# Expert layer of a routed feed-forward block: first product transposed, with its weights streamed per tile as the stationary operand, second matrices resident

## What is computed

```python
k_logits, k_index = jax.lax.top_k(logits, TOPK)
k_prob = jax.nn.softmax(k_logits, axis=-1)
for e in range(E):
    we = jnp.sum(jnp.where(k_index_f == e, k_prob_f, 0.0), axis=-1)
    h = jax.nn.silu(xf @ w1[e] + b1[e]) @ w2[e] + b2[e]
    out = out + we[:, None] * h
x = x + gb * out
```

## Time and profile before

| | us |
|---|---|
| median of 3 runs | 2193.87 |
| lowest and highest of them | 2185.4, 2199.5 |
| span of the profiled execution | 2187.8 |
| experts: from the first DMA issue to the end | 1582.3 to 2187.8 |

### The profile page before, as it was taken

How to read it: one execution, slowest core, us unless ns; L and a number is a source line. 1 busy time by engine, 2 the same in 40 slices (tenths; PEclk the granted TensorE clock), 3 DMA queues, 4 the chain that set the end, 5 groups by cost and what they waited for, 6 DMA issues and landing times. The chain is left out here.

```text
span 2187.8 us, 35435 instructions
## 1 busy us (share of the span) xinstructions
PE 1909.5 (87%) x9314; PEld 1097.2 (50%) x9315; DVE 1300.8 (59%) x2620; ACT 1282.9 (59%) x1387; POOL 357.6 (16%) x383
## 2 busy tenths in 40 slices
PE   2988199898999999989799996699089999999998
PEld 1433044444444444444344445588056667776665
DVE  5543177676877777777577774765234444444443
ACT  4323099898998989989799992244012222222222
POOL 1330200100001000000000003215501111111111
PEclk7988599999999999999899998899589999999999
DMA  3455661506033060521605204622262112222211
GB/s 122 153 171 199 152 152 43 107 10 125 23 71 82 19 130 5 101 52 40 108 5 101 53 6 127 200 116 79 89 190 34 32 31 34 34 34 34 34 31 25
DMA packets 139177, 172.28 MB, mean 79 GB/s; under 512 B 16672, under 2 KB 89248, under 8 KB 138976
## 3 DMA queue, kind: packets, MB, share of 16 engines
q1 hardware_dynamic: 116672, 143.00, 26.6%
q0 software_dynamic: 13824, 19.03, 5.0%
q10 hardware_dynamic: 8608, 9.47, 1.3%
HBM read 106.42 MB, written 65.03 MB: 78 GB/s over the span
## 5 line engine op out<-in xcount | busy, mean ns | idle before, releaser
L771 DVE SCALAR_TENSOR_TENSOR probs<-probs,scal,bil_ps 128x512 f32<-128x512 f32 (+1 forms) x1152 | 773.6, 715 | 278.5 <-ACT probs L734 169.6
L734 ACT ACTIVATE probs<-raw_ps 128x2048 f32<-128x2048 f32 (+1 forms) x288 | 518.7, 1801 | 84.3 <-PE raw_ps L669 84.3
L741 ACT ACTIVATE probs<-probs 128x2048 f32<-128x2048 f32 (+1 forms) x288 | 529.7, 1839 | 34.8 <-DVE probs L771 34.8
L681 PE MATMUL bil_ps<-u_mv,w_st 128*128 128x512 f32 (+3 forms) x1280 | 469.9, 426 | 54.1 <-DVE probs L771 30.8
L1442 ACT ACTIVATE hid_t<-h_tr_ps,b 128x128 f32<-128x128 f32 x576 | 156.3, 383 | 475.7 <-PE h_tr_ps L1406 409.6
L681 PEld LDWEIGHTS bil_ps<-u_mv,w_st 128*128 128x128 f32 x1280 | 217.3, 192 | 410.5 <-DVE probs L771 380.8
L669 PE MATMUL raw_ps<-q_mv,k_st 128*128 128x512 f32 (+3 forms) x1280 | 337.1, 390 | 52.8 <-DMA v_sb<-v_rows 45.1
L696 PE MATMUL o_ps<-probs,v_sb 128*32 128x512 f32 (+3 forms) x2560 | 298.5, 548 | 0.5 <-POOL probs L654 0.5
L669 PEld LDWEIGHTS raw_ps<-q_mv,k_st 128*128 128x128 f32 x1280 | 212.3, 194 | 143.9 <-ACT probs L734 70.1
L1397 PE MATMUL fc_ps<-w,rows_t 128*128 x576 | 262.1, 598 | 1.2 <-issue 0.6
L1417 PE MATMUL fc_ps<-w,hid_t 128*128 x1152 | 260.9, 380 | 1.7 <-DMA b<-in_b 0.9
(11 more groups left out here) (186 smaller groups left out, 1313.7 us busy)
## 6 DMA issues: line engine op xcount, KB each, us to landing
q_mv<-q_split SPq DMA_DIRECT2D x128, 128.0 KB
rows<-x_rows SPq DMA_DIRECT2D x72, 130.0 KB, 2.1
v_rows<-v_st SPq DMA_DIRECT2D x8, 1024.0 KB, 5.2
k_st<-k_split SPq DMA_DIRECT2D x64, 128.0 KB
k_st<-k_split SPq DMA_DIRECT2D x128, 64.0 KB
v_sb<-v_rows SPq DMA_DIRECT2D x32, 256.0 KB
o_t<-o_sb SPq DMA_DIRECT2D x32, 256.0 KB, 2.2
o_t_sb<-o_t SPq DMA_DIRECT2D x32, 256.0 KB, 2.8
```

Of the source, the lines that this page charges most:

```text
L681: mm = pe.matmul(bil_ps[:, hd % 2, column:column + width], w_st[:, kt * P:(kt + 1) * P], u_mv[:, hd, qb * BLK + query:qb * BLK + query + w ...
L734: act.activation(probs[:, s % NBUF, :, first:BLK], raw_ps[:, :, first:BLK], ACT.Tanh).then_inc(tanh_ready, 1)
L741: act.activation(scores, scores, ACT.Exp).then_inc(exp_ready, 1)
L771: dve.scalar_tensor_tensor(scores, scores, scal[:, ALPHA:ALPHA + 1], bil_ps[:, hd % 2, first:BLK], ALU.mult, ALU.add).then_inc(sum_ready, 1)
```

## The change

- **First product.** Eight groups (`hc`) of two matmuls (`k`): the 128x128 piece of `w1` is the stationary operand, the transposed rows (128 columns) are the moving one. The result in `fc1_ps` has the hidden units on partitions, so the eight transposes of `hid`, the copy to `hid` and `h_tr_ps` are gone; SiLU reads `fc1_ps`. The pipeline has three parts instead of four.
- **Weights.** `w2` is loaded whole in the router stage, in the place of `w1`. `w1` is loaded for each tile by SP, 1 MB of the tile's expert, to one of WB = 4 buffers, right behind the tile's rows. SP waits for the first product of tile m-4 besides its waits of before.
- **Buffers.** `fc1_ps` and `fc2_ps` have two buffers each.
- **VectorE's order.** The probabilities of tile m are read right after the copy of `rows_t`, ahead of the sums of tile m-2.
- TensorE's loop holds four steps instead of two.

The diff, cut to its core:

```diff
-            w1v = w1[:, :].rearrange("p (e k n) -> p e k n", e=E, k=KC)
+            w2v = w2[:, :].rearrange("p (e c n) -> p e c n", e=E, c=HID // P)
             for e in range(E):
-                sp.dma_start(w1v[:, e], a["w1"][e].rearrange("(k p) n -> p k n", p=P)).then_inc(w1_in, 16)
+                sp.dma_start(w2v[:, e], a["w2"][e].rearrange("(c p) n -> p c n", p=P)).then_inc(w2_in, 16)
...
+        WB = 4
+        w1 = sb("w1", [P, WB, KC, HID])
-        hid = sb("hid", [P, 2, HID])
-        fc1_ps = ps("fc1_ps", [P, HID])
-        h_tr_ps = ps("h_tr_ps", [P, HID])
-        fc2_ps = ps("fc2_ps", [P, BLK])
+        fc1_ps = ps("fc1_ps", [P, 2, HID])
+        fc2_ps = ps("fc2_ps", [P, 2, BLK])
...
         def _(sp):
                 if active(0):
+                    sp.wait_ge(fc1_mm, m + (FC1_0 - WB + 1))
                     sp.wait_ge(x_tr_mm, m + (XTR_0 - 1))
                     sp.wait_ge(meta_ready, m + (META_0 - 1))
                     row = sp.value_load(tile_row[0:1, ds(m, 1)], min_val=0, max_val=VOID)
                     sp.dma_start(rows[:, u % 2, :], dram["x_rows"][ds(row, P), :]).then_inc(rows_in[u % 2], 16)
+                    e = sp.value_load(tile_expert[0:1, ds(m, 1)], min_val=0, max_val=E - 1)
+                    src = a["w1"].rearrange("e (k p) n -> e p k n", p=P)[ds(e, 1), :, :, :]
+                    sp.dma_start(w1[:, u % WB, :, :], src.rearrange("z p k n -> (z p) k n")
+                                 ).then_inc(w1_in[u % WB], 16)
...
         def _(pe):
                 if active(1):
+                    pe.wait_ge(w1_in[q], (n // WB) * 16 + 16)
                     pe.wait_ge(rows_t_ready, n + (RT_0 + 1))
-                    pe.wait_ge(hid_ready, n + HID_0)
-                    for half in range(HID // BLK):
+                    pe.wait_ge(hid_t_ready, n + (HT_0 - 1))
+                    for hc in range(HC):
                         for k in range(KC):
-                            mm = pe.matmul(fc1_ps[:, half * BLK:(half + 1) * BLK], rows_t[:, p, k * P:(k + 1) * P],
-                                           w1[:, ds(e * (KC * HID) + (k * HID + half * BLK), BLK)],
-                                           start=(k == 0), stop=(k == KC - 1))
+                            mm = pe.matmul(fc1_ps[:, p, hc * P:(hc + 1) * P], w1[:, q, k, hc * P:(hc + 1) * P],
+                                           rows_t[:, p, k * P:(k + 1) * P], start=(k == 0), stop=(k == KC - 1))
...
-                    for hc in range(HC):
-                        tr = pe.transpose(h_tr_ps[:, hc * P:(hc + 1) * P], hid[:, p, hc * P:(hc + 1) * P],
-                                          ident[:, :])
-                    tr.then_inc(h_tr_mm, 1)
-                if active(3):
...
-            skewed(pe, NET, 3, 2, step)
+            skewed(pe, NET, 2, WB, step)
...
         def _(act):
-            for e in range(E):
-                act.dma_start(w2v[:, e], a["w2"][e].rearrange("(c p) n -> p c n", p=P)).then_inc(w2_in, 16)
             act.dma_start(b2[:, :], a["b2"].partition_broadcast(P)).then_inc(w2_in, 16)
...
-                        silu = act.activation(hid_t[:, p, cols], h_tr_ps[:, cols], ACT.Silu,
+                        silu = act.activation(hid_t[:, p, cols], fc1_ps[:, p, cols], ACT.Silu,
...
         def _(dve):
-                    dve.wait_ge(fc1_mm, n + (FC1_0 + 1))
-                    dve.wait_ge(h_tr_mm, n + (HTR_0 - 1))
-                    dve.tensor_copy(hid[:, p, :], fc1_ps[:, :]).then_inc(hid_ready, 1)
```

More of the change, by code:

```diff
@@ L155, in build @@
                          rw1, router_weights, pad_base, tile_first, x_back)
-            stage_router(nc, a, dram, modrow, ident, rows_sb, stats2, rstd2, token_f, blank, w1, w1_in, out,
+            stage_router(nc, a, dram, modrow, ident, rows_sb, stats2, rstd2, token_f, blank, w2, w2_in, out,
                          router_weights, pad_base, tile_first, tile_expert, expert_f, tile_row, pad_row)
-        stage_experts(nc, a, dram, modrow, ident, tile_expert, expert_f, tile_row, w1, w1_in,
+        stage_experts(nc, a, dram, modrow, ident, tile_expert, expert_f, tile_row, w2, w2_in,
                       out)
@@ L984, in _, with stage_router @@
             dve.scalar_tensor_tensor(pairs[:, :, 0], pairs[:, :, 0], -1.0, rstd2[:, :], ALU.mult, ALU.mult)
-def stage_router(nc, a, dram, modrow, ident, rows_sb, stats2, rstd2, token_f, blank, w1, w1_in, out,
+def stage_router(nc, a, dram, modrow, ident, rows_sb, stats2, rstd2, token_f, blank, w2, w2_in, out,
                  router_weights, pad_base, tile_first, tile_expert, expert_f, tile_row, pad_row):
@@ L1328, in stage_experts @@
         x_tr_ps = ps("x_tr_ps", [P, BLK])
-        fc1_ps = ps("fc1_ps", [P, HID])
-        h_tr_ps = ps("h_tr_ps", [P, HID])
-        fc2_ps = ps("fc2_ps", [P, BLK])
+        fc1_ps = ps("fc1_ps", [P, 2, HID])
+        fc2_ps = ps("fc2_ps", [P, 2, BLK])
         rows_in = [sem(f"rows_in{p}") for p in range(2)]
-        b1_in, w2_in = sem("b1_in"), sem("w2_in")
+        w1_in = [sem(f"w1_in{p}") for p in range(WB)]
+        b1_in = sem("b1_in")
         added, y_free = sem("added"), sem("y_free")
@@ L1414, in step @@
                     pe.wait_ge(hid_t_ready, n + (HT_0 + 1))
-                    pe.wait_ge(y_sum_ready, n + YS_0)
+                    pe.wait_ge(y_sum_ready, n + (YS_0 - 1))
                     for hc in range(HC):
-                        mm = pe.matmul(fc2_ps[:, 0:D], hid_t[:, p, hc * P:(hc + 1) * P],
+                        mm = pe.matmul(fc2_ps[:, p, 0:D], hid_t[:, p, hc * P:(hc + 1) * P],
                                        w2[:, ds(e * (HC * D) + hc * D, D)], start=(hc == 0), stop=(hc == HC - 1))
                     mm.then_inc(fc2_mm, 1)
-            skewed(pe, NET, 3, 2, step)
+            skewed(pe, NET, 2, WB, step)
         @block.scalar
@@ L1434, in step @@
             def step(m, u, active):
[L1435 to L1437 removed]
+                if active(1):
+                    n, p = m - 1, (u - 1) % 2
+                    act.wait_ge(fc1_mm, n + (FC1_0 + 1))
                     act.wait_ge(fc2_mm, n + (FC2_0 - 1))
@@ L1441, in step @@
                         cols = slice(hc * P, (hc + 1) * P)
-                        silu = act.activation(hid_t[:, p, cols], h_tr_ps[:, cols], ACT.Silu,
+                        silu = act.activation(hid_t[:, p, cols], fc1_ps[:, p, cols], ACT.Silu,
                                               bias=b1[:, ds(e * HC + hc, 1)])
                     silu.then_inc(hid_t_ready, 1)
-            skewed(act, NET, 2, 2, step)
+            skewed(act, NET, 1, 2, step)
         @block.vector
@@ L1467, in step @@
                     dve.tensor_copy(rows_t[:, u % 2, :], x_tr_ps[:, 0:D]).then_inc(rows_t_ready, 1)
-                if active(1):
-                    n, p = m - 1, (u - 1) % 2
-                    dve.wait_ge(fc1_mm, n + (FC1_0 + 1))
-                    dve.wait_ge(h_tr_mm, n + (HTR_0 - 1))
-                    dve.tensor_copy(hid[:, p, :], fc1_ps[:, :]).then_inc(hid_ready, 1)
[L1473 to L1487, removed]
                     k = u % TR
@@ L1501, in step @@
                                       ).then_inc(meta_ready, 1)
-            skewed(dve, NET, 3, TR, step)
+                if active(2):
+                    n, p, k = m - 2, u % 2, (u - 2) % TR
+                    e = expert_of(n)
+                    dve.wait_ge(meta_ready, n + (META_0 + 1))
+                    dve.wait_ge(y_ready, n + Y_0)
+                    dve.scalar_tensor_tensor(gate[:, :], gates[1], late[:, k:k + 1], gates[0],
+                                             ALU.mult, ALU.add).then_inc(gate_ready, 1)
+                    dve.wait_ge(fc2_mm, n + (FC2_0 + 1))
+                    dve.wait_ge(y_free, n + (FREE_0 - 1))
+                    dve.tensor_tensor(y[:, p, :], fc2_ps[:, p, 0:D], b2[:, ds(e * D, D)], ALU.add
+                                      ).then_inc(y_sum_ready, 1)
+                    dve.wait_ge(gate_ready, n + 1)
+                    dve.wait_ge(y_sum_ready, n + (YS_0 + 1))
+                    dve.scalar_tensor_tensor(y[:, p, :], y[:, p, :], share[:, 1, k:k + 1], gate[:, :],
+                                             ALU.mult, ALU.mult).then_inc(y_ready, 1)
+            skewed(dve, NET, 2, TR, step)
 INPUTS = ["x", "c_t", "wmod", "ident", "scalars", "transforms", "transform_weights", "qkv_wt", "code_wt",
```

30 lines of the change are left out of this document (9 added, 21 removed).

## The result

| | before | after |
|---|---|---|
| median of 4 runs, us | 2190.6 | 2129.05 |
| lowest and highest, us | 2185.4, 2199.5 | 2123.47, 2134.5 |
| span of the profiled execution, us | 2187.8 | 2129.3 |
| experts, from their first DMA issue to the end of the span, us | 605.5 | 544.4 |

The ratio after to before is 0.9725, with an interval of 0.9697 to 0.9754 (the two medians alone give 0.9719, inside it): faster by 2.5 to 3.0%. The forecast was 2130 us.

A forecast was written before the change was run, and what follows sets the result against it. TensorE alone was taken to bound the experts. Start 1591.7, products 504.7, transposes 15.4, clock 1.7 and end 10.9 gave a 2124.4 us span, 63.4 less; off the 2193.9 median, 2130 us (2112 to 2150; 2168 with the accumulation case).

The forecast's parts named there:

- The bound: Experts' steady part: TensorE alone binds, at clock 1.00, with a step of 7.99 us before the change.
- The step: TensorE's step: eight transposes go (-0.87 us), first product takes 3.55 us for 3.44; 7.23 us for 7.99.
- The rivals with a pitch of 0.133 and of 0.19: First product's 32 records: at 0.133 us apart, 2181 us in all (6%); at 0.19, loads unhidden, 2312 us (8%).
- What must stay hidden: Work beside TensorE's step, such as SiLU, y, accumulations, row and weight loads: all stays hidden, cost 0.
- the estimate of 3.3 us a megabyte: Weight stream: 1 MB takes 3.3 us at 316 GB/s; with old traffic 4.9 of 7.23 us, share near 0.68.
- the rival's mechanism: GpSimd's accumulation, delayed some 3.0 us by the weight burst, sets a 7.7 us step: 34 us more, 2164 us; 10%.
- the phase: Within a step: accumulation data move from 3.7 to 6.0 us; weights are issued at 4.6 and move towards their landing.
- The router: Router stage: loading 8 MB of w2 in 1 KB pieces instead of w1 in 4 KB pieces costs 0.
- The start: Start of experts: first product of tile 0 at 1591.7 us (1593.4 before), its second near 1601 instead of 1614.4.
- My 1.7: First product of tile 0: TensorE's lower clock of 1.2 GHz adds 1.7 us over the steady one.
- The end: From the last matmul to the end of the span: 10.9 us, where it was 10.0 before.
- The sum: Whole kernel: 2124.4 us of span, 63.4 less than 2187.8; taken off the median of 2193.9, 2130 us.

The follow-up runs named there:

- 2 MB: Changed kernel with each w1 tile loaded twice, the second time to buffers that TensorE waits for but doesn't use: 2123.7 us, the experts 545.8.
- a full collision: Changed kernel with each w1 tile issued when the y of an earlier tile is ready, so its 1 MB moves during that accumulation: 2120.8 us.
- 2.5 MB: Changed kernel with each tile's weights loaded twice and half of them a third time, to an unread DRAM buffer: 2187.67 us, the experts 580.5.
- The two runs with a better start: Changed kernel with the first four w1 tiles loaded in the router stage: ratio to before 0.9727; the same with b2 moved behind tile 1's transposes: 0.9752.
- the yardstick: The changed kernel again, unaltered, on two occasions: 2139.14 and 2135.96 us, ratios to before 0.9706 and 0.9727.

## Why the prediction was right, point by point

**The bound.** TensorE's step sets the experts, before and after, without a gap and at clock 1.00. Shown by the profile after, and by the run with the old product, whose step is that of before.

**The step.** Forecast 0.22 + 3.55 + 3.46 = 7.23, measured 0.22 + 3.57 + 3.46 = 7.25. The pitch of the 32 records is 0.1116 us where 0.111 was taken. The 64-column run shows that it is the load, and not the streaming (0.107), that sets this pitch, and so that the reading of the earlier trace rows and of the loads in the earlier trace rows (0.110 and 0.113) was sound, while the 0.133 from the matmul row was too high, as suspected. The rivals with a pitch of 0.133 and of 0.19 are excluded: in a run of 32 as in one of 4 the next load begins before the record of the one before it ends, and only 0.004 us of each stand out over the streaming. The 0.76 x 72 = 55 us of the forecast are the 53 to 56 between the old and the new product.

**What must stay hidden.** Costed at nothing, and the run without the stream confirms it to about 1 us. The margin was mis-sized on both sides: the estimate of 3.3 us a megabyte made 2 MB impossible, and they fit. But the rival's mechanism is real. It is the accumulation's landing, one at a time on GpSimd, that ends the room: 4.0 us with the stream as placed, 6.0 under a full collision, 5.7 with 2 MB, 6.7 with 2.5 MB. The reason given against it, the phase (issues 2.2 us apart), isn't needed: the collision costs 2.0 us, not 3.0, and 6.9 us of GpSimd still fit in 7.25. The Trainium skill (DMA: Bandwidth & Descriptors, section Queues, rings and completion order) has a DMA engine drain a packet of some 9 to 17 descriptors of one queue before it turns to the next. The prediction concluded from it that an accumulation stands behind most of a burst each time it meets one; the collision bears that out in part, with 2.0 of some 3.3 us.

**The router.** Costed at 0, and right (188.2 us without the load of `w2`, 187.4 with it, see above), though the transfer did change. `w2` in pieces of 1 KB kept SP's queue busy issuing for 30.46 us where 18.98 were needed for `w1`, and by 1440 it was over, as in the earlier trace rows; the windows after:

```profile
1420.00:1440.00 20.00, 19.22 (x141) 15.68 (x140) 11.42 (x22) 9.31 (x13) 0.00 (x0) 0.95 1.10 348
1440.00:1460.00 20.00, 19.33 (x146) 16.02 (x145) 12.86 (x45) 9.11 (x14) 0.00 (x0) 1.00 0.02 7
```

**The start.** Forecast: the first product 9.4 us into the stage, measured 9.6, but the wait was only in part the one forecast. I had the product wait for its weights, issued 2.7 us into the stage and landing in 6.5 us; they were issued at 2.6 and landed in 6.2, at 8.8 us. What came last was the transposes of tile 1, which I had left out: their rows queued behind these weights and landed 0.3 us after them. The rows of tile 0 took over 4 us to land beside `b2`, not 2.1. The two runs with a better start are worth 2 us each, but the first takes away the wait for the weights and the wait for the rows of tile 1 together. The lower clock of the first product cost 2.4 us where 1.7 was taken: its record is 6.16 us long, and 3.74 at a granted clock of 1.00 (5.03 and 5.58 in the yardstick's two profiles, so this varies). My 1.7 had mixed the length of a run (5.20) with a distance of the chain (3.44); by lengths the cost before was 1.6 (5.20 for 3.60).

**The end.** Forecast 10.9 us from the last matmul to the end of the span, measured 10.8 (2118.45 to 2129.3).

**The sum.** 2124.4 us of span forecast, 2129.3 measured. Of the 4.9, 2.6 are a later start of the stage: 2.0 in stages whose code wasn't changed, 0.6 in the router (182.4 us from SP's store to the experts for 181.8), where the other profiles differ by more. Then 1.4 are the step (72 x 0.02), 0.7 the first product's clock and 0.2 its later start; the end gives 0.1 back. Against the median the errors cancelled, with a median of before 3 us lower than the one I started from. The forecast of 2130 for 2129.05 is closer than its working deserves.

## What to carry to other kernels

A product that leaves its result in the layout which the next one needs saves the transposes whole where TensorE is the bound, even if it multiplies the weight loads by four, as long as each load (here 0.112 us for 128x128 of fp32, two records a matmul) has about as much streaming beside it (128 columns, 0.107 us): the longer of the two sets the pace, so compute both before turning operands round. Split such a change into its parts, here some 55 us for the product and 7 for the placement, and read small parts from the stage, not from the whole time. When a new stream fits the DMA engines on average, look at the one transfer that is awaited one at a time: its landing is the margin.

## What the runs showed that I had not expected

- The DMA share is no fraction of 1: 326 GB/s at 0.96, 350 at 1.10, 373 at 1.03, the last with part of the traffic from DRAM to DRAM. The kernel before has 410 GB/s at 1.03 from 1420 to 1430 us, while it loads `w1`, so 373 is no ceiling either.
- In the run with 64 moving columns the granted clock was at its lower level (0.50, 1.2 GHz) for some 19 us, from 1590.0 to past 1609, in which TensorE was never idle: two first products, and most of the second product of tile 0. In the changed kernel, with 128 columns, it rose within the first product (0.50 up to 1599, 1.00 from 1600). It is one run, and why the clock rose later wasn't tested. Windows of it:

```profile
1590.00:1600.00 10.00, 9.97 (x48) 9.98 (x48) 2.11 (x11) 1.51 (x6) 0.00 (x0) 0.50 0.83 299
1600.00:1610.00 10.00, 10.00 (x37) 8.94 (x37) 0.15 (x1) 2.84 (x11) 0.00 (x0) 0.54 0.35 118
1610.00:1620.00 10.00, 10.00 (x76) 9.44 (x74) 3.92 (x15) 2.18 (x8) 1.89 (x2) 1.00 0.47 131
```

  A first product of 6.93 us, twice, and a second of 6.11 us, where the changed kernel has 6.16, 3.74 and 3.62, make 6.5 of the 7 us by which its stage is longer. In the steady part, where first and second products alternate, the clock stays at 1.00.
